# Decoder layer with experts: the second bias as one float32r product of split rows, with the gate weights split on GpSimd

## What is computed

```
def _moe(h, w_gate, we1, be1, we2, be2):
    x = h.reshape(-1, d)
    raw = softmax(x @ w_gate)                     # 4 experts
    top_vals, top_idx = top_k(raw, 2)
    w = softmax(top_vals)
    comb = zeros((t, E)).at[arange(t)[:, None], top_idx].add(w)
    hmid = gelu(einsum('td,edi->tei', x, we1) + be1[None])
    eout = einsum('tei,eid->ted', hmid, we2) + be2[None]
    out = einsum('te,ted->td', comb, eout)
```

## Time and profile before

| | |
|---|---|
| median of 3 runs | 1186.73 us (1185.58 to 1187.6) |
| profiled execution, its own time | 1184.21 us |
| its span in the trace | 1182.4 us |
| TensorE busy | 1113.7 us, 94% of the span |
| VectorE busy | 954.8 us, 81% |
| ScalarE, GpSimd busy | 669.1 us and 661.2 us, 57% and 56% |
| chain that ended last, by engine | TensorE 56%, VectorE 14%, issue 6%, GpSimd 4%, ScalarE 2% |

### The profile page before, as it was taken

How to read it: one execution, slowest core, us unless ns; L and a number is a source line. 1 busy time by engine, 2 the same in 40 slices (tenths; PEclk the granted TensorE clock), 3 DMA queues, 4 the chain that set the end, 5 groups by cost and what they waited for, 6 DMA issues and landing times.

```text
span 1182.4 us, 30629 instructions
## 1 busy us (share of the span) xinstructions
PE 1113.7 (94%) x11732; PEld 920.0 (78%) x11732; DVE 954.8 (81%) x2219; ACT 669.1 (57%) x1703; POOL 661.2 (56%) x714
## 2 busy tenths in 40 slices
PE   6899999799999999888999999999999999999997
PEld 5667666566666766556899899999999899988887
DVE  6768877887878878867788888888888888868977
ACT  5466564577777777564555444444444444558663
POOL 4467564645555555264778554444544455737665
PEclk9899999999999999989999999999999999999999
DMA  5875544354444444302111000000000100101111
GB/s 160 212 185 132 128 125 112 97 138 123 126 121 131 119 126 126 104 21 89 61 66 55 1 1 1 1 1 1 1 1 1 37 2 1 37 19 36 37 37 36
DMA packets 107491, 83.05 MB, mean 70 GB/s; under 512 B 74172, under 2 KB 95804, under 8 KB 107346
## 3 DMA queue, kind: packets, MB, share of 16 engines
q1 hardware_dynamic: 107345, 81.10, 24.6%
HBM read 57.02 MB, written 23.07 MB: 68 GB/s over the span
## 4 chain that ended last, share of the span: by engine, by line
PE 56%; DVE 14%; issue 6%; POOL 4%; ACT 2%; SPq 1%; DMA 0%; POOLq 0%; DVEq 0%; ACTq 0%
PE bank L1632 5%; PE bank L1633 5%; PE bank L1634 5%; PE bank L1688 4%; PE bank L1661 4%; PE bank L663 4%; PE bank L641 3%; PE bank L560 3%; DVE B_nr L803 2%; PE bank L1648 2%; PE bank L1703 2%; PE bank L1701 2%; PE bank L1702 2%; PE bank L1649 2%; PE bank L1650 2%
## 5 line engine op out<-in xcount | busy, mean ns | idle before, releaser
L1936 POOL TENSOR_TENSOR C_QK<-C_t1b,C_t2b 128x512 f32<-128x512 f32 x128 | 168.8, 1319 | 227.2 <-DVE C_t2b L1775 226.6
L1772 DVE SCALAR_TENSOR_TENSOR C_t1b<-bank,C_bcol,C_tabs 64x512 f32<-64x512 f32 x256 | 192.0, 750 | 38.4 <-PE bank L1634 34.3
L803 DVE TENSOR_REDUCE B_nr<-bank 128x4 f32<-128x512 f32 x256 | 164.3, 684 | 24.3 <-PE bank L602 23.8
L1062 ACT ACTIVATE PT<-bank 128x512 f32<-128x512 f32 x224 | 130.1, 596 | 92.4 <-PE bank L641 90.8
L1632 PE MATMUL bank<-C_XTh,C_Wh 128*128 128x512 f32 x256 | 112.4, 439 | 5.7 <-DVE C_XTl L1621 1.9
L1868 ACT ACTIVATE C_P<-bank,C_nm 128x128 f32<-128x128 f32 x256 | 90.7, 367 | 34.2 <-DVE C_nm L1785 32.6
L1887 ACT ACTIVATE C_V<-bank 128x512 f32<-128x512 f32 x64 | 38.1, 597 | 124.1 <-PE bank L1650 122.5
L1633 PE MATMUL bank<-C_XTl,C_Wh 128*128 128x512 f32 x256 | 101.7, 397 | 0.0
L1634 PE MATMUL bank<-C_XTh,C_Wl 128*128 128x512 f32 x256 | 101.2, 395 | 0.0
L663 PE MATMUL bank<-PT,vpool 128*32 128x128 f32 x2048 | 97.1, 285 | 2.0 <-ACT OTf L1072 2.0
L1775 DVE SCALAR_TENSOR_TENSOR C_t2b<-bank,C_bcol,C_tabs 128x512 f32<-128x512 f32 x128 | 96.1, 751 | 1.8
(11 more groups left out here) (271 smaller groups left out, 3495.8 us busy)
## 6 DMA issues: line engine op xcount, KB each, us to landing
Adrq<-PB SPq DMA_DIRECT2D x16, 192.0 KB, 3.0
Adrk<-PB SPq DMA_DIRECT2D x16, 192.0 KB, 3.2
stk<-Adrq SPq DMA_DIRECT2D x16, 192.0 KB
stk<-Adrk SPq DMA_DIRECT2D x16, 192.0 KB
Bdrq<-PB SPq DMA_DIRECT2D x16, 192.0 KB, 3.0
stk<-Bdrq SPq DMA_DIRECT2D x32, 96.0 KB
Bdrk<-PB SPq DMA_DIRECT2D x16, 192.0 KB, 2.8
stk<-Bdrk SPq DMA_DIRECT2D x32, 96.0 KB
```

Of the source, the lines that this page charges most:

```text
L803: e.tensor_reduce(dst, bank[n % 2][:, :].rearrange("p (a b) -> p a b", a=4), AX.X, ALU.max, negate=True).then_inc(sem("m_dve"), 1)
L1062: e.activation(pt_of(n)[:, :], bank2(n)[:, :], ACT.Exp).then_inc(sem("e_act"), 1)
L1772: e.scalar_tensor_tensor(out=v4(t1b[kq][lo:lo + 64, :]), in0=v4(o[hi:hi + 64, :]), scalar=bc[hi:hi + 64, :], in1=tabsC[hi:hi + 64, 2 * kq ...
L1936: e.tensor_tensor(QK[v % 3][:, kq, :], t1b[kq][:, :], t2b[kq][:, :], ALU.add).then_inc(sem("rc_pool"), 1)
```

## The change

The second bias is made by one float32r product for each block. The contraction has 128 rows, of which 16 were used; now three groups of 16 rows are: weights' high part x table's high part (rows 0 to 15), weights' low part x table's high part (rows 32 to 47), and weights' high part x table's low part (rows 64 to 79).

- The host writes the table `Db2` three times, at rows 0, 32 and 64. When stage D opens, ScalarE copies it to a float32r tile `D_b2r` (128x1024 numbers) as its first instruction there, and VectorE then replaces rows 64 to 95 by the low part (32x1024 numbers) as its first instruction.
- VectorE writes the gate weights into a small tile of their own, `D_combS`. GpSimd sets the 128x128 tile to zero for chunks 0 and 1 (VectorE did so), copies the weights' high part to two places (128x32), and writes the low part (128x16). This is `comb_pool`. For chunk 0 it stands behind GpSimd's first residual sum (`D_X`, L2316 before); for chunk c = 1 to 3 in step 7, behind `layernorm_power` of the last block of chunk c-1.
- `comb_t_pe` now waits for GpSimd's last operation of `comb_pool` and not for VectorE's L2183. It stands in the same place on TensorE. `D_combT` is float32r.

```diff
     def comb_t_pe(e, q, c):
-        q.wait_ge("gate_dve", 18 * (c + 1))
+        q.wait_ge("comb_zero", min(c, 1) + 1 + 2 * (c + 1))
         o = dturn_bank(q, ("ct", c))
...
-            q.wait_ge("ld_b2", 16)
+            q.wait_ge("ld_b2", 18)
...
-                    e.matmul(ebank(c, b, x)[:, 256:512], combT[i][:, :], b2[:, b, :], start=True, stop=True)
+                    e.matmul(ebank(c, b, x)[:, 256:512], combT[i][:, :], b2r[:, b, :], start=True, stop=True)
...
-            if c < 2:
-                e.memset(comb128[c][:, :], 0.0).then_inc(sem("comb_zero"), 1)
...
+    def bias_act(e, q):
+        q.wait_ge("ld_b2", 16)
+        e.activation(b2r[:, :, :], b2[:, :, :], ACT.Copy).then_inc(sem("ld_b2"), 1)
+
+    def bias_dve(e, q):
+        low = slice(64, 96)
+        q.wait_ge("ld_b2", 17)
+        e.tensor_tensor(b2r[low, :, :], b2[low, :, :], b2r[low, :, :].bitcast(F32), ALU.subtract).then_inc(sem("ld_b2"), 1)
+
+    def comb_pool(e, q, c):
+        T = comb128[c % 2]
+        if c < 2:
+            e.memset(T[:, :], 0.0).then_inc(sem("comb_zero"), 1)
+        n = min(c, 1) + 1 + 2 * c
+        flat = comb[c % 2][:, :, :].rearrange("p a b -> p (a b)")
+        copies = T[:, :].rearrange("p (k r) -> p k r", k=2)[:, :, 0:16].bitcast(F32R)
+        q.wait_ge("comb_zero", n)
+        q.wait_ge("gate_dve", 18 * (c + 1))
+        if c >= 2:
+            q.wait_ge("ct_pe", c - 1)
+        e.tensor_copy(copies, flat.unsqueeze(1).to_broadcast([128, 2, 16])).then_inc(sem("comb_zero"), 1)
+        q.wait_ge("comb_zero", n + 1)
+        e.tensor_tensor(T[:, 32:48], flat, T[:, 0:16], ALU.subtract).then_inc(sem("comb_zero"), 1)
...
         residual(0, 0)
+        comb_pool(e, q, 0)
         for c in range(1, NCH):
             for m in range(8):
...
                 if m < 3:
                     residual(c - 1, m + 1)
+                if m == 7:
+                    comb_pool(e, q, c)
```

More of the change, by code:

```diff
@@ L1470, in program @@
     b2 = sb("D_b2", [128, 4, 256], F32, st_d)
+    b2r = sb("D_b2r", [128, 4, 256], F32R, st_d)
     XF.append(sb("D_XF1", [128, 2, 512], F32, st_d))
@@ L1485, in program @@
     comb128 = [sb(f"D_comb{i}", [128, 128], F32, st_d) for i in range(2)]
-    comb = [T[:, 0:16].rearrange("p (a b) -> p a b", a=4) for T in comb128]
-    combT = [sb(f"D_combT{i}", [128, 128], F32, st_d) for i in range(2)]
+    comb = [sb(f"D_combS{i}", [128, 4, 4], F32, st_d) for i in range(2)]
+    combT = [sb(f"D_combT{i}", [128, 128], F32R, st_d) for i in range(2)]
     X2 = [sb(f"D_X2{i}", [128, 4, 256], F32, st_d) for i in range(2)]
@@ L2181, in gate_dve @@
             q.wait_ge("gate_dve", n + 17)
-            q.wait_ge("comb_zero", min(c, 1) + 1)
+            if c >= 2:
+                q.wait_ge("comb_zero", 2 + 2 * (c - 1))
             e.tensor_tensor(comb[c % 2][:, :, :], ew[:, :, :], bc(mx[:, :]), ALU.mult).then_inc(sem("gate_dve"), 1)
@@ L2227, in finish @@
             layernorm_apply(e, q, X[:, j, :], yD[j % 2][:, :], j, "fn", 4, 4).then_inc(sem("f_dve"), 1)
+        bias_dve(e, q)
         for c in range(1, NCH):
@@ L2275, in comb_t_act @@
         e.activation(combT[c % 2][:, :], dbank(("ct", c))[:, 0:128], ACT.Copy).then_inc(sem("ct_act"), 1)
+    def bias_act(e, q):
[14 more added lines that the diff above has]
+        q.wait_ge("gate_dve", 18 * (c + 1))
+        if c >= 2:
+            q.wait_ge("ct_pe", c - 1)
+        e.tensor_copy(copies, flat.unsqueeze(1).to_broadcast([128, 2, 16])).then_inc(sem("comb_zero"), 1)
+        q.wait_ge("comb_zero", n + 1)
+        e.tensor_tensor(T[:, 32:48], flat, T[:, 0:16], ALU.subtract).then_inc(sem("comb_zero"), 1)
     def act_d(e):
         q = Queue(e, sem)
+        bias_act(e, q)
         for c in range(1, NCH):
@@ L2495, in layouts @@
     for b in range(4):
-        f["Db2"][4 * b:4 * b + 4, b, :] = g("be2").reshape(4, 256)
+        for k in range(3):
+            f["Db2"][32 * k + 4 * b:32 * k + 4 * b + 4, b, :] = g("be2").reshape(4, 256)
     f["x"] = np.asarray(a["x"])
```

## The result

The changed kernel takes 1199.11 us (median of 6 runs, 1197.02 to 1201.58), the kernel before 1184.77 us in 6 runs beside it (1183.03 to 1187.6). The ratio is 1.0124, with a 95% interval from 1.0107 to 1.0141: 14.3 us slower. One of the ten runs with the product only took 1734.51 us, in a slow state, and changes their median by under 0.1 us. The forecast was 13.3 us slower. The span of the profiled execution is 1197.3 us, and 1182.4 before.

What follows compares the result with a forecast made beforehand. VectorE has the path in the two chunks ahead, TensorE close behind; TensorE bounds chunk 3's hidden work. Waits of 8.5 us plus 4.8 for the clock make 13.3, on 1186.73 giving 1200.0 us, range 1193.5 to 1206.

Steps and rivals of the forecast that it cites:

- The saving: Stage D bias products: 0.31 us less TensorE time for each of 16 blocks, 5.0 in all, counting only where TensorE bounds.
- The sign that the prediction gave for it: Profile after: one bias record per block, 0.24 us from the product ahead to the second one behind.
- The waits: Four borders: gate-weight transposes wait for GpSimd's split behind `rstd`, TensorE standing still 4.1, 2.3, 1.9 and 4.6 us.
- losses at full clock: Lateness from the waits at the four borders, clock staying full: 2.9, 1.9, 1.3 and 2.35 us, sum 8.5.
- The one term that was off: First border: TensorE idles 4.1 us for GpSimd's split, VectorE's next start is 2.9 us late.
- rival (b): Clock falls at all four borders, 15 to 21 us; includes VectorE-GpSimd contention, about 1 us at the first border; chance 0.13.
- The GpSimd operations: GpSimd's split: 0.2, 0.25 and 0.3 us taken for its three operations; with hand-overs 0.6, or 0.95 with the MEMSET.
- What hides the table: First border: VectorE's added table work is hidden under the transpose's wait; without that wait it would cost 2.3 us.
- The clock: TensorE at half clock behind border gaps: three falls, each 3.3 us long and delaying 1.6, 4.8 us in all.
- the shortest of the six gaps: Profiled trace before: of six TensorE gaps of 1.7 to 2.9 us, the shortest followed by half clock, lasting 3.3 us.
- The time: Whole kernel: 13.3 us slower, added to the median before of 1186.73, gives 1200.0 us.

Runs made afterwards that it cites:

- product only: Kernel before with one float32r product of rounded weights and rounded table, both low parts left out: 1186.15 us against 1185.96, ratio 1.0001.
- all waits filled: Changed kernel with idle products (18, 7, 5 and 20) on TensorE in all four transpose waits: 1193.75 us against 1184.67 before, ratio 1.0075.
- the two kernels without the wait: Changed kernel with four splits moved, table split at stage opening or in the end of stage C: 1188.33 and 1186.52 us; first border 5.95 and 3.79.
- three splits moved: Changed kernel with GpSimd's split for chunks 1 to 3 moved ahead of `rstd` in step 7: 1193.36 us against 1185.96 before, ratio 1.0067.
- four splits moved with the early table: Four splits moved, plus the bias table split in the end of stage C: 1186.52 us against 1183.47 before, ratio 1.0025.
- the filled pair: Changed kernel with idle products on TensorE in the waits at the first and fourth border (18 and 19): 1194.58 us against 1183.47 before, ratio 1.0099.
- the wait only: Changed kernel with the float32 bias product and full float32 table, GpSimd's split and the transposes' waits kept: 1199.0 us against 1185.96 before, ratio 1.0110.
- all of it early: Changed kernel with four splits moved, the last to step 6, and the table split in stage C: 1185.37 us against 1184.67 before, ratio 1.0000.
- four splits moved: As three splits moved, plus chunk 0's split ahead of its last `D_HL`; table still split at stage opening: 1188.33 us against 1185.96 before, ratio 1.0026.

## Why the prediction was right

**The saving.** Forecast 0.31 us a product, and that it counts in few places. Measured 0.32 (0.67 to 0.35 us) a product. (The sign that the prediction gave for it, 0.24 us from the product ahead to the second one behind, was a slip: by its own figures that is three steps of 0.12, 0.36.) It won 0.66 us between the second border and the tail with the product alone, and nothing in the tail, which does not start late in that kernel.

**The waits.** Forecast gaps of 4.1, 2.3, 1.9 and 4.6 us; measured 4.84, 1.88, 1.55 and 5.19. Forecast losses at full clock of 2.9, 1.9, 1.3 and 2.35, sum 8.5; measured, with all waits filled, 3.8, 1.7, 1.2 and 2.3, sum 9.1. The one term that was off is the first. The contention between VectorE's subtraction and GpSimd stood in rival (b) with "about 1 us on top at the first border"; it belonged in the sum. The residual sum took 1.70 us and not 0.73. The GpSimd operations were cheaper than I took them: 0.20 for MEMSET, 0.21 and 0.22 for copy and subtraction, with hand-overs 0.77 and not 0.95 us.

**What hides the table.** Forecast: hidden under the first wait, 2.3 us if the wait goes. Measured: 5.95 - 3.79 = 2.2 us between the two kernels without the wait.

**The clock.** Forecast: 4.8 us, three falls at 1.6. Measured: 5.0 us, from two falls: 2.65 in the tail (25.54 to 22.89), and at the first border 1.8 up to VectorE's first sum of block 0 (9.58 to 7.80) and 0.6 behind it, in the column "to 2nd" (30.10 to 29.50). That these 0.6 us belong to the first fall is seen in VectorE's first sums of blocks 0 and 1 of chunk 0. In the changed kernel:

```profile
1091.15 0.43 DVE L2196 TENSOR_TENSOR D_y<-bank,D_X 128x256 f32<-128x256 f32 x1 [3.56 <-PE bank L2118]
...
1099.05 0.42 DVE L2196 TENSOR_TENSOR D_y<-bank,D_X 128x256 f32<-128x256 f32 x1 [1.88 <-PE bank L2118]
```

and with all waits filled:

```profile
1090.02 0.42 DVE L2198 TENSOR_TENSOR D_y<-bank,D_X 128x256 f32<-128x256 f32 x1 [1.73 <-PE bank L2120]
...
1097.20 0.41 DVE L2198 TENSOR_TENSOR D_y<-bank,D_X 128x256 f32<-128x256 f32 x1
```

They lie 7.90 us apart and 7.18, and only at half clock does VectorE wait for TensorE at block 1; the last stretch, from block 3 to VectorE's start behind the second border, is the same (7.90 and 7.92). The sum of 4.8 was right by luck, by two errors in opposite directions: two falls and not three, each at some 2.5 us and not 1.6. Both lasted about 6.8 us in this trace (the first from 1086.8 to 1093.6), and I had taken 3.3, the length behind the shortest of the six gaps. Of the first, 1.8 us show at VectorE's next start, 4.75 us behind the transpose and not 2.92 (with all waits filled); the rest shows a block later.

**The time.** 1200.0 us stood against 1199.11, but the median before was 1186.73 in the runs that I had and 1184.77 in the six that it is compared with. That the times agree within 0.9 us is therefore luck in part. By difference it is 13.3 against 14.3.

Of my expectations of the runs, four missed: three splits moved, four splits moved with the early table, and by under 1 us the filled pair and the wait only. With all of it early, the medians' +0.7 lies just above the range and the ratio's 0.0 in it. With four splits moved the time was met and the mechanism was not. The two that missed by more and this one had one reason, which my own rule should have caught: for a wait on an engine that works in order, everything ahead of the awaited instruction counts, not only the last wait ahead of it.

## What to carry to other kernels

A small operation that is given to an engine with time to spare starts when that engine comes to it, not when its operands are ready. Here GpSimd idled 31.3 us behind one kind of wait, and four pairs of operations of 0.2 us, three of them put behind that wait, cost 13 us (wait only). Look at what stands ahead of the place, and put the work where the operands have just come; then ask what it saves, which here was 5 us of an engine that was 94% busy, and nothing of the time.

## What the runs showed of the hardware

All gaps of TensorE of 3.9 to 5.2 us in stage D, 11 in seven traces, were followed by the half clock. Of eleven gaps of 1.5 to 2.0 us, in six traces, six were (one of five of 1.52 to 1.56 us, five of six of 1.65 to 2.00), and the same place in the same code went either way. Behind 25 gaps of 0.9 to 1.3 us in stage D it never fell. The half clock held for one of two times: about 3.4 us in all six falls behind the shorter gaps and in three behind the long ones (3.89, 4.14 and 4.14 us), about 6.8 us in the other eight. The Trainium skill, "TensorE: Matmul & The Clock Gate", section "Why this matters for your kernels", advises against idle gaps between bursts of matmuls, because the clock falls back behind them. These runs agree, and show it behind gaps as short as 1.56 us.

GpSimd's first sum over 128x256 in stage D took 1.70 to 1.72 us beside VectorE's subtraction with two SBUF inputs (six traces), and 0.73 to 0.75 in the six traces in which no such subtraction stands there. That agrees with what the Trainium skill says of GpSimd's SBUF interfaces ("GPSIMD Engine Reference", section "Specifications"), that they are shared with VectorE, with contention where a VectorE instruction has two SBUF inputs; here it is GpSimd that takes longer.

A float32 product over 256 columns costs 0.43 us in a row of products, a float32r one 0.12.
